# Two routed FFNs around an attention: one-hots of the first routing by row tile, and W2's split copies moved into the first tiles

## The reference

```
x = x + 0.5 * ffn(layernorm(x))       # routed FFN
x = x + attention(layernorm(x))       # 8 heads of 128, 512 keys shared by all rows
x = x + 0.5 * ffn(layernorm(x))       # the same routed FFN, same weights

ffn(x): e = argmax(x @ gate_w.T + gate_b + expert_bias)    # one of 8 experts for each row
        relu(x @ w1[e] + b1[e]) @ w2[e] + b2[e]            # 128 -> 512 -> 128
```

## Time and profile before

| | |
|---|---|
| median of 3 runs | 743.93 us |
| the profiled execution | 751.08 us, span 749.3 us |
| TensorE | busy 711.1 us (95%) |
| VectorE | 603.0 us (80%) |
| ScalarE | 496.9 us (66%) |
| GpSimd | 363.2 us (48%) |
| first 140 us / attention 140 to 680 / rest: TensorE busy | 127.2 of 140 / 529.4 of 540 / 54.6 of 69 |

### The profile page before, as it was taken

The page is one execution under the profiler, slowest core; times in us unless marked ns, Lnnn a source line. Parts: engine busy times, 40 slices in busy tenths (PEclk is TensorE's granted clock), DMA queues, the critical chain, the costliest instruction groups (busy, mean ns, idle before and its releaser), DMA issues.

```text
span 749.3 us, 15246 instructions
## 1 busy us (share of the span) xinstructions
PE 711.1 (95%) x4374; PEld 595.9 (80%) x4374; DVE 603.0 (80%) x1648; ACT 496.9 (66%) x1212; POOL 363.2 (48%) x496
## 2 busy tenths in 40 slices
PE   8979899999999999999999999999999999989992
PEld 7758797778888888878878888887887887769991
DVE  6979898887787878878788787788878787788882
ACT  3676677678677677667667767766766775546660
POOL 5056787343334445346345444544634633576662
PEclk9999999999999999999999999999999999999996
DMA  9932342200000000000000000000000011232210
GB/s 249 339 143 42 93 85 74 63 19 1 1 1 1 1 5 12 1 2 14 1 1 12 5 2 8 8 0 1 16 1 1 16 43 57 100 87 63 58 47 5
DMA packets 31792, 31.49 MB, mean 42 GB/s; under 512 B 5049, under 2 KB 26183, under 8 KB 31200
## 3 DMA queue, kind: packets, MB, share of 16 engines
q1 hardware_dynamic: 27360, 23.91, 10.7%
q0 software_dynamic: 3520, 6.40, 3.3%
q10 hardware_dynamic: 832, 0.21, 0.1%
HBM read 20.96 MB, written 10.47 MB: 42 GB/s over the span
## 4 chain that ended last, share of the span: by engine, by line
PE 75%; DVE 13%; issue 3%; DMA 3%; POOL 2%; ACT 1%; another core or an unknown queue 0%; DVEq 0%; POOLq 0%; SPq 0%; ACTq 0%
PE bank L1449 16%; PE bank L1451 15%; PE bank L1450 15%; PE bank L1660 13%; PE bank L1496 5%; PE bank L1484 3%; DVE neg_max L1334 2%; DVE probsT_lo L1340 2%; PE bank L1499 2%; DVE hT_lo L1192 1%; DMA rows<-in_L_attn_x 1%; POOL rows L561 1%; PE bank L1506 1%; DVE h L1171 1%; PE bank L1592 1%
## 5 line engine op out<-in xcount | busy, mean ns | idle before, releaser
L577 POOL TENSOR_SCALAR probs<-probs,row_inv 128x512 f32<-128x512 f32 x256 | 177.8, 695 | 274.2 <-DVE row_inv L1345 263.4
L786 ACT ACTIVATE probs<-bank,neg_max 128x512 f32<-128x512 f32 x256 | 176.1, 688 | 144.3 <-DVE neg_max L1334 143.2
L1334 DVE TENSOR_REDUCE neg_max<-bank 128x1 f32<-128x512 f32 x256 | 176.5, 690 | 86.7 <-PE bank L1451 83.4
L1340 DVE TENSOR_TENSOR probsT_lo<-bank,probsT_hi 128x512 fp32r<-128x512 f32 x256 | 174.3, 681 | 2.2 <-ACT probsT_hi L795 2.0
L1660 PEld LDWEIGHTS bank<-ident,probs 128*128 128x128 f32 x1024 | 127.2, 140 | 38.4 <-issue 1.7
L1660 PE MATMUL bank<-ident,probs 128*128 128x128 f32 x1024 | 153.4, 272 | 1.7 <-POOL probs L577 1.3
L795 ACT ACTIVATE probsT_hi<-bank 128x512 fp32r<-128x512 f32 x256 | 150.8, 589 | 2.1 <-PE bank L1660 2.1
L1449 PE MATMUL bank<-m_hi,xT_hi 128*128 128x512 f32 x256 | 122.4, 478 | 0.0
L1449 PE MATMUL bank<-probsT_hi,vw_hi 128*128 128x512 f32 x256 | 101.7, 397 | 3.4 <-DVE probsT_lo L1340 3.4
L1450 PE MATMUL bank<-probsT_lo,vw_hi 128*128 128x512 f32 x256 | 101.5, 396 | 0.0
L1451 PE MATMUL bank<-probsT_hi,vw_lo 128*128 128x512 f32 x256 | 101.4, 396 | 0.0
(11 more groups left out here) (220 smaller groups left out, 1237.0 us busy)
## 6 DMA issues: line engine op xcount, KB each, us to landing
b<-in_L_ffn_b SPq DMA_DIRECT2D x4, 1024.0 KB
x_packed<-slot_rows SPq DMA_DIRECT2D x39, 65.5 KB
slot_rows<-slots SPq DMA_DIRECT2D x39, 65.5 KB
x_stats<-rows SPq DMA_DIRECT2D x4, 524.0 KB, 10.0
rows<-x_packed SPq DMA_DIRECT2D x8, 262.0 KB, 2.7
rows<-in_L_attn_x SPq DMA_DIRECT2D x4, 512.0 KB, 8.3
w_lo<-in_L_ffn_w SPq DMA_DIRECT2D x8, 256.0 KB, 7.4
w_hi_lo<-in_L_ffn_w SPq DMA_DIRECT2D x8, 256.0 KB, 5.7
```

The lines of the kernel that those rows point to most:

```text
L577: pool.tensor_scalar(PR[:, u % 4, :], PR[:, u % 4, :], RI[:, u % 4:u % 4 + 1], 1.0, ALU.mult, ALU.mult).then_inc(normed, 1)
L786: act.activation(PR[:, n % 4, :], BK[n % 2][:, :], ACT.Exp, bias=NM[:, n % 4:n % 4 + 1], accum_out=SU[:, n % 4:n % 4 + 1]).then_inc(probs, 1)
L1334: v.tensor_reduce(NM[:, n % 4:n % 4 + 1], BK[n % 2][:, :], AX.X, ALU.max, negate=True)\
L1340: v.tensor_tensor(PTL[at], BK[2 + u % 2][:, :].rearrange("p (c q) -> p c q", c=KC), PTH[at].bitcast(fp32), ALU.subtract).then_inc(pT_lo, 1)
```

## The change

- `OHL` becomes a tile of its own name that shares its memory with W2HL; it uses the high halves of experts 0 to 3 there, so `w2_high` of these stands behind the placement products. XS is cleared whole by GpSimd's memset instead of its last part.
- `low_onehots(c)`: eight tensor_scalar instructions, one for each row tile, each comparing with LOF and multiplying by VAL (both f32, one scalar per partition). `slot_onehots(c)` loses its multiplication.
- `count_tiles` of the first routing takes the maximum of the count and 1, so every expert has a tile and tile j's expert is at most j.
- ScalarE: `w2_high(0)` between tile 0's norm and step 0, then 1, 2 in step 0; 3, 4 in step 1; 5, 6, 7 in steps 2, 3, 4. VectorE: `half_b2` and `w2_low(0)` in step 0; 1, 2 in step 1; 3, 4 in step 2; 5, 6, 7 in steps 3, 4, 5; `packed_rows` in step 5. TensorE waits for w2_lo one expert at a time in steps 4 to 11.
- SyncE: b1's second half behind b2.

Changed lines, without context (numbers of before, after):

```diff
@@ -69,6 +69,9 @@
+        with ExitStack() as onehots_at:
+            OHL = sb("onehot_low", [P, E * FC, 2, 2, P], fp16, onehots_at)
@@ -132,15 +135,14 @@
-            LOF = sb("rank_low", [P, T], fp16, prep)
+            LOF = sb("rank_low", [P, T], fp32, prep)
-            VAL = sb("row_code", [P, T], fp16, prep)
-            OHLX = sb("onehot_low_rest", [P, CH, P], fp16, prep)
+            VAL = sb("row_code", [P, T], fp32, prep)
@@ -180,9 +182,6 @@
-        OHL = [XS[:, :, :].rearrange("p r w -> p (r w)").bitcast(fp16)[:, c * CH * P:(c + 1) * CH * P]
-               .rearrange("p (t q) -> p t q", t=CH) for c in range(NCH - 1)] + [OHLX[:, :, :]]
@@ -344,6 +343,11 @@
+        W2_HIGHS = {0: [1, 2], 1: [3, 4], 2: [5], 3: [6], 4: [7]}
+        W2_LOWS = {0: [0], 1: [1, 2], 2: [3, 4], 3: [5], 4: [6], 5: [7]}
@@ -399,9 +403,9 @@
-            load_b1(1)
+            load_b1(1)
@@ -479,7 +483,7 @@
-            pool.memset(XS[:, R - 1, :], 0.0)
+            pool.memset(XS[:, :, :], 0.0)
@@ -697,8 +701,6 @@
-            for e in range(4):
-                w2_high(e)
@@ -754,8 +756,9 @@
-                        w2_high(4 + 2 * m)
-                        w2_high(5 + 2 * m)
+                    if r == 0 and m in W2_HIGHS:
+                        for e in W2_HIGHS[m]:
+                            w2_high(e)
@@ -771,6 +774,8 @@
+                if r == 0:
+                    w2_high(0)
@@ -916,9 +921,12 @@
-                v.tensor_tensor(OHL[c], IOT[:, :].unsqueeze(1).to_broadcast([P, CH, P]),
-                                LOF[:, CH * c:CH * c + CH].unsqueeze(2).to_broadcast([P, CH, P]),
-                                ALU.is_equal).then_inc(low_ready, 1)
+                for i in range(CH):
+                    t = CH * c + i
+                    last = v.tensor_scalar(OHL[:, t // 2, 0, t % 2, :], IOT[:, :], LOF[:, t:t + 1], VAL[:, t:t + 1],
+                                           ALU.is_equal, ALU.mult)
+                last.then_inc(low_ready, 1)
@@ -929,10 +937,10 @@
-            def count_tiles(r, total, first, i):
+            def count_tiles(r, total, first, i, least=0):
-                    link(v.tensor_scalar(CNTI[:, 0, :], total, float(first), None, ALU.add), step, count)
+                    link(v.tensor_scalar(CNTI[:, 0, :], total, float(least), float(first), ALU.max, ALU.add), step, count)
@@ -957,7 +965,7 @@
-                    count_tiles(0, total0, P - 1, i)
+                    count_tiles(0, total0, P - 1, i, 1)
@@ -970,11 +978,9 @@
-                over = lambda b: b[:, own].unsqueeze(2).to_broadcast([P, CH, SLOTS])
-                v.tensor_tensor(OHS[c], IOT[:, 0:SLOTS].unsqueeze(1).to_broadcast([P, CH, SLOTS]), over(SIDX),
-                                ALU.is_equal).then_inc(place_step, 1)
-                dve.wait_ge(place_step, c + 1)
-                v.tensor_tensor(OHS[c], OHS[c], over(VAL), ALU.mult).then_inc(place_ready, 1)
+                v.tensor_tensor(OHS[c], IOT[:, 0:SLOTS].unsqueeze(1).to_broadcast([P, CH, SLOTS]),
+                                SIDX[:, own].unsqueeze(2).to_broadcast([P, CH, SLOTS]), ALU.is_equal)\
+                    .then_inc(place_ready, 1)
@@ -984,9 +990,9 @@
-                dve.wait_ge(place_step, NCH + 2)
+                dve.wait_ge(place_step, 2)
-                dve.wait_ge(place_step, NCH + 3)
+                dve.wait_ge(place_step, 3)
@@ -1108,9 +1114,6 @@
-            half_b2()
-            w2_low(0)
-            w2_low(1)
@@ -1196,10 +1199,12 @@
-                    if r == 0 and m < 3:
-                        for e in range(2 + 2 * m, 4 + 2 * m):
+                    if r == 0 and m == 0:
+                        half_b2()
+                    if r == 0 and m in W2_LOWS:
+                        for e in W2_LOWS[m]:
-                    if r == 0 and m == 3:
+                    if r == 0 and m == 5:
@@ -1440,7 +1445,7 @@
-                    last = pe.matmul(BK[PLACE_BANK][:, 0:SLOTS], OHL[c][:, i, :], OHS[c][:, i, :],
+                    last = pe.matmul(BK[PLACE_BANK][:, 0:SLOTS], OHL[:, t // 2, 0, t % 2, :], OHS[c][:, i, :],
@@ -1484,8 +1489,8 @@
-                    if m == 4 and r == 0:
-                        pe.wait_ge(w2_lo, E)
+                    if r == 0 and 4 <= m < 4 + E:
+                        pe.wait_ge(w2_lo, m - 3)
```

## The result

| | before | after |
|---|---|---|
| median of the runs, us | 743.72 (741.9 to 749.73, 20 runs) | 746.93 (743.97 to 751.52, 20 runs) |
| ratio | | 1.004 [1.0023, 1.0058] |
| profiled execution, us (span) | 751.08 (749.3) | 746.15 (744.4) |
| tile 0's transpose on TensorE | 44.15 | 44.31 |
| tile 7's | 64.39 | 66.64 |

The change is 0.4% slower, 3.2 us, where I forecast 1.7 faster. The spans of the two profiled executions say the opposite. At the start of the second FFN, which the diff doesn't touch, two tile steps took 4.38 and 4.03 us in the execution of before and 2.51 and 2.91 in that of after, and other executions differ there as much (from 2.92 to 6.86 for the longest). So spans are not compared. I compare tile 7's transpose with tile 0's.

A forecast was written before the change was run, and what follows sets the result against it. TensorE, 95% busy, was taken as the bound. Norm 1.0 us earlier and head 6 1.1 shorter, less 0.4 lost in steps 3 to 5, made -1.7 us: 742.2 from 743.93, range 740.2 to 744.8.

The forecast's parts named there:

- Part 1: VectorE's one-hots as eight tensor_scalars 0.23 us apart, 2.25 a chunk: placement 0.76 us later, costing up to 0.8 us alone.
- (a): Rival on VectorE: one-hots are cheap, 0.11 to 0.13 us apart, placement 1.0 earlier; -2.8 us, 741.1; chance 0.18.
- (d): Rival on VectorE: slower, one-hots 0.32 us apart, a chunk 2.97, placement 3.7 later; +1.3 us, 745.2; chance 0.13.
- the gather: Tile 0's gather, landing at 42.0 to 43.2, so that tile 0's norm starts at 42.6 against 43.6, 1.0 us earlier.
- rival (c): A transfer takes ScalarE's place: tile 0's gather lands at 43.4, norm gains 0.2 us; -0.9 us, 743.0; chance 0.12.
- I take none: No fall of TensorE's clock behind the shorter idle before tile 0, so head 6 gains 1.1 us.
- rival (b): TensorE's clock falls all the same behind tile 0's idle, head 6 stays at 3.86 us; -0.6 us, 743.3; chance 0.15.
- The sum: Tile 7's transpose on TensorE at 62.7 instead of 64.39: -1.7 us.
- packed_rows makes a step of 3.9: VectorE's step 5 with a whole tile's work, w2_low(7) and packed_rows takes 3.85 us, ending at 60.0.
- Is it kept?: Whether the gain lasts behind tile 7: tile 16's stall of 3.12 us moves unchanged, its phase worth -1.5 to +0.5 us.
- the line for slower: The chance given to a slower outcome, above 745.4 us: 0.12.

The follow-up runs named there:

- experiment 1: Each part of the change alone against the kernel before: one-hots alone, ratio 0.9996; moved W2 copies with the new load order alone, ratio 1.0033.
- experiment 8: Changed kernel with one per-partition scalar instead of two in each one-hot, row code multiplied into the slot one-hot again; one execution only, 758.43 us.
- experiment 4: Changed kernel with b1's second half loaded only once tile 0's gather has landed; ratio to before 0.9974.
- experiment 3: 26 warm-up products instead of 6 ahead of tile 0: in the changed kernel 0.9992, in before 0.9957; changed kernel unchanged beside them 1.0015 (ratios to before).

## Why the prediction was wrong

**Part 1 held.** Foreseen 300 ns, 0.23 apart, a chunk 2.25; measured 303 ns, 0.22, 2.19 (28.92 less 26.73). The last placement products start 0.43 later, 0.76 foreseen. With the one-hots alone the time did not change by more than the noise (experiment 1). Rivals (a) and (d) are out. The Trainium skill (VectorE: DVE Perf Modes, the perf-mode tier table) gave 0.22 by four elements a cycle for 16 bits, and the trace agrees; it gives no price for the scalars, and experiment 8 shows that with one of the two fewer the op stands at 0.16.

**The first step that failed, the gather: rival (c)'s mechanism was true.** Foreseen to land at 42.0 to 43.2, it let the norm start at 43.76, where I had 42.6 and (c) 43.4. I had dated the hidden landing of before, 42.7, by counting the queue's packets up to one gather's 32. In after the same count passes 32 by 42.5 (9 and 29), and the norm still had to wait until 43.76. Some of these packets may be the next gather's, whose issue began at 39.44; in either case the count doesn't date a landing. My other reason was that shorter packets would stand in front of it. But b1's second half is only moved behind b2, and 0.96 us of the wait was its packets (experiment 4). The four copies that left ScalarE had stood in this wait and had cost next to nothing there. Their removal brought nothing: tile 0's transpose is at 44.31, not 43.15, 1.16 late.

**The second step that failed, "I take none": rival (b)'s fall came, twice, and was under-priced.** I ruled a fall out by one row, an idle time of 1.96 at 85.81 with no fall behind it. That was too little to go by. Seven kernels had a fall behind waits of 2.08 to 2.99 in front of tile 0, one had none behind 2.38, and after's second fall (56.17) stands behind no wait over 1.01. And the wait stayed long because the gather held it; with the gather early it was 1.06 and had no fall behind it (experiment 4). Nor did I see what a slower clock does here. I took 1.1 us of head 6; the first fall cost 1.70 and the second 0.85. Slow products delay ScalarE's evacuations, and its two copies and xT_hi stand behind these, in before as in after. But in before VectorE has w2_low and half_b2 for much of that time, 5.32 us busy in 44 to 52 against 3.78; in after it idles, 1.6 us longer than without a fall, and is short by that later. This fits the ramps: 20.24 with one fall and 20.20 with two in before's order (experiment 1), 21.48 and 22.33 here. No run has before's order without a fall, so what a fall costs there isn't measured. I priced the falls as TensorE's loss, where it is VectorE that comes out late.

**The sum.** I forecast tile 7 at 62.7, it came at 66.64, 3.94 late. 1.16 is the gather. My steps from 43.15 to 62.7 are 19.55, and the same order without a fall measured 19.78: 0.23, so the arithmetic of the steps was near. The remaining 2.55 is that kernel against the one with two falls (22.33). In VectorE's terms, where I had it full from 51.75 and through step 5 at 60.0, it was full from 54.29, and packed_rows (62.04) ended near 63.5. With both failed steps undone (experiment 4: gather early, no fall) tile 7 came at 63.11 and the ratio was 0.9974, where the forecast is 0.9977 (742.2 to 743.93); its interval [0.994, 1.0008] holds no gain as well. That packed_rows makes a step of 3.9 I had; that it could stand in front of the tiles at no cost to the ramp, in a gap of VectorE that the trace of before shows (2.19 us for b2, ended at 44.98), I had not looked at. The chances had a slip too: half of (d) is 0.065, and the line for slower has 0.12.

**Is it kept?** Not fully: tile 16's stall shrank by 1.2 and the lag at tile 38 was 0.71 us (137.94 against 137.23). The 3.2 us of the medians are more than this one execution shows behind the ramp. In experiment 3's comparison the unchanged kernel was 1.0015 [0.9986, 1.0044], and its executions show where one kernel's times part: in its trace a fall from 670.10 to 676.93 stands in the second FFN, and a tile step there took 6.86 us, where after's trace has no fall and no step over 2.91 at that place. Its 12 runs have a median clock of 0.9855 against 0.987 of before's, and 0.001 of clock goes with 0.75 us in them (correlation -0.84), so falls could make up that small difference. For the 3.2 us it stays open: over after's own 20 runs clock and time hardly go together (correlation -0.37), and the clocks of before's runs beside them are not on record.

## What to carry to other kernels

Before work is moved off an engine because it is first in the chain, look at what ends second there: copies that stood in a transfer's wait were nearly free, and after the move they were not (ramps of 21.39 and 21.48 against 20.24, one fall each). Put work that has no consumer soon (packed_rows here) into a gap in front of a pipeline and not into the steps where its engine is full: the ramp gained 1.8 us by it, though no run shows the time gained by that alone. And where one engine's clock may fall, follow the fall through every queue behind it before it is called cheap.

## What the runs showed of the hardware

A wait of TensorE in front of tile 0 brought a fall behind it in seven kernels with 2.08 (after) to 2.99 us (packed_rows in step 3), none in three with 2.38 (packed_rows first), 1.69 and 1.06, and none behind the 1.96 of before at tile 16: of these the shortest had none, the longer ones mostly one, and 2.38 against 2.08 shows that the length is not all. Two executions of the changed kernel fell at 45.93 and 56.17, and at 45.46 and 65.94. The Trainium skill (TensorE: Matmul & The Clock Gate, What's actually happening) has the slow phase of a kernel's start vary from run to run with the same code; these two traces show the like in mid-kernel. Twenty or more warm-up products filled into the wait kept the clock up behind it in all six kernels that had them. Ahead of the end of the program, most falls in these traces lasted 3.4 us, and four lasted 6.8.

A gather of 32 packets beside large queued loads waits for them even where its own engine has issued it: issued from 37.88 on, its queue moved nothing before 41.5. With 1 MB deferred it moved 30 packets by 41, and tile 0's norm started at 42.80 instead of 43.76.

A per-partition scalar costs VectorE 55 ns an instruction (303 to 248 ns at 128x128 of 16 bits), a quarter of the 0.22 from start to start.
